# Attention values in split passes over two batches and two heads, with the context sums stored in DRAM between

## The reference

```
q = rmsnorm(layernorm(x) @ Wq); k = rmsnorm(ctx @ Wk); v = ctx @ Wv
attn = softmax(q k^T / sqrt(128)); out = (attn @ v) @ Wo
x = x + out
x = x + ffn(layernorm(x))      # Hadamard rotation, 8-bit activations, ternary weights
```

## Time and profile before

| | us |
|---|---|
| median of 3 runs (1493.36 to 1501.02) | 1493.83 |
| the profiled execution's own time | 1490.84 |
| its span | 1489.1 |
| PE busy in the span | 1419.2 (95%) |
| ACT busy | 986.5 (66%) |
| DVE busy | 940.7 (63%) |
| POOL busy | 521.8 (35%) |

### The profile page before, as it was taken

How to read it: one execution, slowest core, us unless ns; L and a number is a source line. 1 busy time by engine, 2 the same in 40 slices (tenths; PEclk the granted TensorE clock), 3 DMA queues, 4 the chain that set the end, 5 groups by cost and what they waited for, 6 DMA issues and landing times. The chain is left out here.

```text
span 1489.1 us, 30811 instructions
## 1 busy us (share of the span) xinstructions
PE 1419.2 (95%) x9026; PEld 1222.3 (82%) x9026; DVE 940.7 (63%) x2592; ACT 986.5 (66%) x2223; POOL 521.8 (35%) x323
## 2 busy tenths in 40 slices
PE   6999989999999999999999999998699999999996
PEld 6888869999999989899899899997566777677763
DVE  5312046667777777677677777766466777677764
ACT  5556658888888888788788788887434344434442
POOL 0033325422323323332233222235245555455533
PEclk9999989999999999999999999999899999999998
DMA  7767622344434344334333334334611112112100
GB/s 243 215 176 201 192 69 81 102 118 119 113 110 113 112 128 114 102 118 121 118 112 111 109 113 128 102 85 142 216 50 36 42 56 70 42 42 56 49 8 15
DMA packets 160329, 158.26 MB, mean 106 GB/s; under 512 B 83585, under 2 KB 134801, under 8 KB 158417
## 3 DMA queue, kind: packets, MB, share of 16 engines
q1 hardware_dynamic: 153296, 144.40, 34.2%
q10 hardware_dynamic: 6912, 12.59, 2.7%
HBM read 123.44 MB, written 33.14 MB: 105 GB/s over the span
## 5 line engine op out<-in xcount | busy, mean ns | idle before, releaser
L695 POOL TENSOR_TENSOR rk_sp<-ms_sp,neg_half 76x10 f32<-76x10 f32 (+1 forms) x128 | 241.9, 1911 | 605.8 <-DMA ms_sp<-ms 605.8
L848 ACT ACTIVATE k_hi<-psK 128x362 fp32r<-128x362 f32 x256 | 120.5, 471 | 116.6 <-PE psK L729 114.6
L860 ACT ACTIVATE ex<-sc,nb,rq 100x361 f32<-100x361 f32 x256 | 175.6, 686 | 31.7 <-DVE nb L1023 30.3
L729 PE MATMUL psK<-cT_hi,wk_hi 128*128 128x362 f32 x512 | 170.8, 334 | 1.1 <-DVE k_lo L984 1.1
L729 PE MATMUL psK<-cT_hi,wk_lo 128*128 128x362 f32 x512 | 169.0, 330 | 0.0
L729 PE MATMUL psK<-cT_lo,wk_hi 128*128 128x362 f32 x512 | 168.9, 330 | 0.0
L995 DVE TENSOR_TENSOR pT_lo<-psP,pT_hi 121x300 fp32r<-121x300 f32 x256 | 120.4, 470 | 73.8 <-ACT pT_hi L875 69.8
L867 ACT ACTIVATE pr<-ex,ri 100x361 f32<-100x361 f32 x256 | 153.0, 598 | 13.7 <-PE psP L764 13.6
L1016 DVE CUSTOM_DVE_ANT_0 sc<-psS,rk 100x361 f32<-100x361 f32 x256 | 135.5, 529 | 19.4 <-PE psS L753 13.6
L776 PE MATMUL psZ<-pT_hi,cK_hi 120*128 120x400 f32 (+1 forms) x384 | 143.1, 373 | 0.1
L984 DVE TENSOR_TENSOR k_lo<-psK,k_hi 128x362 fp32r<-128x362 f32 x256 | 135.7, 530 | 8.6 <-ACT sq L854 8.6
(11 more groups left out here) (172 smaller groups left out, 3530.9 us busy)
## 6 DMA issues: line engine op xcount, KB each, us to landing
rk<-rk_dram SPq DMA_DIRECT2D x64, 564.1 KB
o_in<-o_dram SPq DMA_DIRECT2D x13, 1024.0 KB, 5.8
q_dram<-q_out SPq DMA_DIRECT2D x64, 200.0 KB, 4.3
q_in<-q_dram SPq DMA_DIRECT2D x64, 200.0 KB, 4.8
o_dram<-o SPq DMA_DIRECT2D x64, 200.0 KB, 5.3
stage<-in_w_ff SPq DMA_DIRECT2D x12, 1024.0 KB, 6.1
w_in<-in_w_ff ACTq DMA_DIRECT2D x48, 256.0 KB, 3.0
cT_in<-in_ctxT SPq DMA_DIRECT2D x16, 361.0 KB, 4.9
```

The costliest lines, as they stand in the source:

```text
L695: nc.gpsimd.tensor_tensor(rk_sp[:, cols], ms_sp[:, cols], neg_half[0:HG * SKR, :].to_broadcast([HG * SKR, n]), op=ALU.pow).then_inc(g_rk, 1)
L729: last = nc.tensor.matmul(psK[h % 2][:, 0:SKP], w[:, c, col:col + D], x[:, slot, c, :], start=(n == 0), stop=(n == 3 * CC - 1))
L848: nc.scalar.activation(k_hi[:, j, h, :], psK[h % 2][:, 0:SKP], ACT.Copy)
L860: nc.scalar.activation(ex[:, h % 2, :], sc[:, h % 2, :], ACT.Exp, bias=nb[:, h % 2:h % 2 + 1], scale=rq[:, j % 2, h:h + 1], accum_out=rs[: ...
```

## The change

The values are computed as three F32R passes, from z and Wv both split. For all units but those of the last two batches (`STORED = 56` units), z no longer goes straight to PE. It is stored to a DRAM tensor `z_dram`, ordered by pair of batches, head, partition and batch. When both batches of a pair are stored, each unit of the next pair (8 units, `PAIR`) loads two heads of both batches (`z_in`, 128 x 800), splits them (`z_hi`, `z_lo`), and one matmul covers 200 columns: one head, two batches. The last 8 units are split and multiplied for one batch and four heads, 100 columns at a time, beside the last 6 stored ones; there the code is written with other places (`late(u)`, from unit 58 on). Wv is loaded and split in two pieces in the first group of `queries`, with the stage buffer that the other weights use. Some memory is shared to make room (`squares_mem`), and `dynamic_dma_scratch_size` is set to 512.

The core of the diff:

```diff
+    z_dram = nc.dram_tensor("z_dram", [B // 2 - 1, H, P, 2, CC * SQ], F32, kind="Internal").ap()
...
-        SPLIT_AT = {0: 1, 2: 2, 4: 3, 8: 4, 10: 5}
+        SPLIT_AT = {0: 1, 2: 2, 4: 3, 8: 4, 10: 5, 12: 6, 14: 7}
...
-                        if h == 9:
-                            sp.dma_start(wv_sb[:], wv.rearrange("(c p) n -> p c n", p=P)).then_inc(d_wv, 16)
+                        if h in (9, 11):
+                            load_piece(6 + h // 2 - 4)
...
-        z = sb("z", [P, CC, UQ])
+        z = sb("z", [P, HG, CC, SQ])
+        z_in = sb("z_in", [P, 2, 2, CC, SQ])
+        z_hi, z_lo = (sb(n, [P, 2, 2, CC, SQ], F32R) for n in ("z_hi", "z_lo"))
...
+        def z_free(eng, w):
+            if isinstance(w, int) and w > STORED:
+                eng.wait_ge(v_zlo, of_unit(w - 1) + 1)
+            elif due(w):
+                eng.wait_ge(d_z, w * 16)
...
+            def store_z(u, pair, k):
+                dst = z_dram[bass.ds(held(sp, pair), 1), k % NG * HG:(k % NG + 1) * HG, :, k // NG, :].rearrange("a h p n -> p (a h) n")
+                done = held(sp, u + 1)
+                sp.wait_ge(a_z, done)
+                sp.wait_ge(v_z, done)
                 apart(sp, sp_passed)
-                sp.dma_start(dst, o[:, j % 2, :].rearrange("p (h q) -> p h q", q=SQ)).then_inc(d_o[j % 2], 16)
...
+            def load_z(u, pair, k):
...
+                stored = held(sp, pair * (PAIR * 16) + (NG + k // 2 + 1) * 16)
+                used = held(sp, of_pair(u - 1) + 1)
+                first = isinstance(u, int) and u == PAIR
+                sp.wait_ge(d_z, stored)
+                apart(sp, sp_passed)
+                if not first:
+                    sp.wait_ge(v_zlo, used)
+                apart(sp, sp_passed)
+                sp.dma_start(z_in[:].rearrange("p h b c q -> p h (b c q)"), src).then_inc(d_zin, 16)
...
+                if real(u - 2, STORED):
+                    store_z(u - 2, pair + (k - 2) // PAIR, (k - 2) % PAIR)
+                if not late(u) and real(u + 2 - PAIR, STORED):
+                    load_z(u + 2, pair + (k + 2) // PAIR - 1, (k + 2) % PAIR)
                 if real(u + 2, UNITS):
                     load_q(u + 2, b + (j + 2) // NG, (j + 2) % NG)
                     spread_rk(u + 2, j % 2)
-                if real(u - 2, UNITS):
-                    store_o(u - 2, b + (j - 2) // NG, (j - 2) % NG)
+                if late(u) and real(u + 2 - PAIR, STORED):
+                    load_z(u + 2, pair + (k + 2) // PAIR - 1, (k + 2) % PAIR)
+                if real(u - PAIR, STORED):
+                    store_pair(u, pair - 1, k)
+                if late(u):
+                    store_unit(u - 2, b + (j - 2) // NG, (j - 2) % NG)
...
+            def values(e, heads, width):
+                pe.wait_ge(v_zlo, e + 1)
+                if due(e):
+                    pe.wait_ge(a_o, e)
...
+                for i, head in enumerate(heads):
+                    first = True
                     for c in range(CC):
-                        last = nc.tensor.matmul(psV[:, h * SQ:(h + 1) * SQ], wv_sb[:, c, col:col + D],
-                                                z[:, c, h * SQ:(h + 1) * SQ], start=(c == 0), stop=(c == CC - 1))
-                    if h == HG - 1:
-                        last.then_inc(p_v, 1)
...
+                        for w, x in ((wv_hi, hi), (wv_hi, lo), (wv_lo, hi)):
+                            last = nc.tensor.matmul(psV[:, i * width:(i + 1) * width], w[:, c, head * D:(head + 1) * D],
+                                                    x[:, i, :, c, :], start=first, stop=(c == CC - 1 and w is wv_lo))
+                            first = False
+                last.then_inc(p_v, 1)
...
+                    if h == 0 and real(u - PAIR, STORED):
+                        values(of_pair(u), (2 * k, 2 * k + 1), 2 * SQ)
+                    if h == 2 and late(u):
+                        values(of_unit(u - 2), range((j - 2) % NG * HG, (j - 2) % NG * HG + HG), SQ)
...
             def copy_z(u):
                 act.wait_ge(p_z, u * CC + 1)
-                if due(u):
-                    act.wait_ge(p_v, u)
-                nc.scalar.activation(z[:, 0, :], psZ[0][:, 0:UQ], ACT.Copy).then_inc(a_z, 1)
+                z_free(act, u)
+                nc.scalar.activation(z[:, :, 0, :], psZ[0][:, 0:UQ].rearrange("p (h q) -> p h q", q=SQ), ACT.Copy).then_inc(a_z, 1)
...
+            def high_z(e, part):
+                if due(e):
+                    act.wait_ge(p_v, e)
+                nc.scalar.activation(z_hi[:].rearrange("p h b c q -> p (h b c q)"), part, ACT.Copy).then_inc(a_zhi, 1)
...
+                    if h == 0 and late(u):
+                        high_unit(u - 2)
+                    if h == (3 if late(u) else 0) and real(u + 1 - PAIR, STORED):
+                        high_pair(u + 1)
...
+                    if h == 1 and late(u):
+                        low_z(of_unit(u - 2), z[:].rearrange("p h c q -> p (h c q)"))
+                    if h == (3 if late(u) else 2) and real(u + 1 - PAIR, STORED):
+                        low_z(of_pair(u + 1), z_in[:].rearrange("p h b c q -> p (h b c q)"))
```

More of the change, by code:

```diff
@@ L171, in queries @@
             pieces.append((wk.rearrange("(c p) n -> p c n", p=P)[:, :, cols], wk_hi[:, :, cols], wk_lo[:, :, cols]))
+        for j in range(2):
+            cols = slice(j * KWD, (j + 1) * KWD)
+            pieces.append((wv.rearrange("(c p) n -> p c n", p=P)[:, :, cols], wv_hi[:, :, cols], wv_lo[:, :, cols]))
         halves = [slice(k * QW // 2, (k + 1) * QW // 2) for k in range(2)]
@@ L294, in squares @@
                     rows = slice(j * QW32, (j + 1) * QW32)
-                    last = nc.tensor.matmul(psS[rows, 0:GT], sel[:, QW32 - 1 - k:2 * QW32 - 1 - k], sq[:, k % 2, j, :],
+                    last = nc.tensor.matmul(psS[rows, 0:GT], sel[:, QW32 - 1 - k:2 * QW32 - 1 - k], sq[k % 2][:, j, :],
                                             start=(k == 0), stop=(k == NG - 1), tile_position=(0, j * QW32))
@@ L517, in attention @@
     CHUNKS = 3 * WC * FF // DIM
+    STORED = UNITS - 2 * NG
+    PAIR = 2 * NG
     with ExitStack() as ctx:
@@ L521, in attention @@
         cT_in, cK_in = weights["cT_in"], weights["cK_in"]
-        cT_hi, cT_lo, ones = (weights[k] for k in ("cT_hi", "cT_lo", "ones"))
+        cT_hi, cT_lo = (weights[k] for k in ("cT_hi", "cT_lo"))
         cK_hi, cK_lo = sb("cK_hi", [P, 2, 3, CD], F32R), sb("cK_lo", [P, 2, 3, CD], F32R)
@@ L573, in pipeline, with batch, late, of_pair @@
         def pipeline(eng, unit):
-            def batch(b, par):
+            def batch(pair, par):
+                b = pair * 2 + par
                 for j in range(NG):
-                    unit(b * NG + j, b, j, par)
+                    unit(b * NG + j, b, j, par, pair)
             for b in range(-1, 4):
-                batch(b, b % 2)
+                batch(b // 2, b % 2)
             with eng.Fori(2, B // 2 - 1) as pair:
[L582 to L585, removed]
+                batch(pair, 0)
+                batch(pair, 1)
+            batch(B // 2 - 1, 0)
+            batch(B // 2 - 1, 1)
             for j in range(2):
-                unit(UNITS + j, B, j, 0)
+                unit(UNITS + j, B, j, 0, B // 2)
+        LAST_ONE = STORED + 2
+        def late(u):
+            return isinstance(u, int) and u >= LAST_ONE
+        def of_pair(u):
+            return u - PAIR if not late(u) else LAST_ONE - PAIR + 2 * (u - LAST_ONE)
+        def of_unit(w):
+            return of_pair(min(w + 2, UNITS - 1)) + 1 + max(w + 3 - UNITS, 0)
+        def z_free(eng, w):
[3 more added lines that the diff above has]
+                eng.wait_ge(d_z, w * 16)
         def first_batch(b):
@@ L644, in unit @@
+            def unit(u, b, j, par, pair):
                 if j == 0 and real(b, B - 1):
@@ L817, in unit @@
                         gather(u - 1, (j - 1) % NG, par if j else 1 - par, h - 2)
-            nc.tensor.matmul(psV[:, 0:3], ones[:], asums[:], start=True, stop=True).then_inc(p_sum, 1)
+            pe.wait_ge(g_ones, 1)
+            nc.tensor.matmul(psV[:, 0:3], o[:, 0, 0:P], asums[:], start=True, stop=True).then_inc(p_sum, 1)
             pipeline(pe, unit)
```

129 lines of the change are left out of this document (78 added, 51 removed).

## The result

The changed kernel takes 1711.82 us (median of 4 runs, 1705.77 to 1714.29) against 1493.93 for the one before on the same chip: 1.144 times the time, 95% interval 1.1417 to 1.1464. Predicted were 1664 us and 1525 to 1730. The profiled execution has a span of 1711.2 us, 222.1 more than before.

A forecast was written before the change was run, and what follows sets the result against it. It took the two-unit ring through z's store to bound the kernel at 16.15 us a unit. 1489.1 + 148 + 13 + 6 + 3 = 1659, plus 1.7 and 3.0, gave 1664 us; range 1525 to 1730.

The forecast's parts named there:

- The value matmul: On PE, 12 records of 200 columns at 0.112 us in a stored unit: 1.34 us instead of 1.79, 0.45 less.
- the line: Record distances on PE at 256 and 512 columns, extended down to 200 columns: 0.094 us a record.
- The rival of slow short passes: One-pass matmuls of 200 columns on PE take some 0.39 us each, giving 1726 us; chance 0.06.
- the ring: Z's copy, split, load, SP chain, store and landing: 32.3 us over two units, 16.15 each, +148 us; chance 0.72.
- The landing of the store: On SP's queue, the 400 KB store of z was taken to need 5.9 us to land.
- PE stays the bound: Z's copy never waits and PE bounds: 1470 us at 0.094 a record, 1493 at 0.112; chances 0.08 and 0.04.
- The turn-taking rival: Stores land in time; alternating ACT and DVE bound units at 13.5 us, 35 more, 1528 us; chance 0.10.
- The last units: Units 58 to 63 pay 2.2 us each on PE, 13; two half-empty units behind them add 6.
- The start: In the first group of queries, two more splits of Wv wait for staged loads: 3 us, bounds 0 and 10.

The follow-up runs named there:

- e2: Changed kernel with only the store of z moved, from behind SP's whole chain to between the issue of ms_sp and the wait for POOL: 1626.8 us.
- e3: Changed kernel with the store of z issued by ACT at head 1 on ACT's own DMA queue: 1638.4 us.
- e4: Changed kernel with z's load behind the rk chain, both splits of z at the end of head 3, and z's store ahead of the POOL wait: 1727.7 us.
- e11: The kernel before the change with 4 of 8 value matmuls left in each unit: 1482.8 us, ratio 0.990–0.993.
- e9: e8 with 4 of the 12 value matmuls left in each two-batch pass: 1596.5 us.
- e8: e5 with load_z moved from behind the rk chain to behind the early store, ahead of SP's wait for POOL: 1586.0 us.
- e10: e8 with load_z put back behind the rk chain for the last eight units alone: 1566.0 us.
- e12: e10 with the stored pairs' high and low splits on POOL at h = 2, in all but the last units: 1536.4 us.
- e7: Changed kernel with 8 of the 24 value matmuls left in each one-batch pass of the last eight units: 1684.8 us.
- e5: e4 with ACT's high split of the stored pair moved to the start of head 3: 1597.1 us.
- e6: e2 with ACT's high split of the stored pair at the start of head 3, for the last eight units only: 1621.9 us.

## Why the prediction was right, and where not

**The value matmul: right.** 0.112 us was taken for 200 columns, against 0.094 by the line; measured 0.111. The same pace at 100 and at 200 columns says what rows of before could not: the moving columns do not set it. What these records have in common is the load of 128 x 128 weights; that this load sets the pace is argued, not shown by itself. The rival of slow short passes (0.39 us) is out. Its sum had a slip that matters: 4.7 - 1.8 is 2.9 us a unit and not 3.2, which makes 1711 us, the measured time. So the time alone could not have told it from the ring; the distances of the records and e2 do. The Trainium skill, TensorE: Matmul & The Clock Gate, section LDWEIGHTS (loading the stationary operand), estimates 107 ns for such a load; the trace agrees at 2.4 GHz with 0.111 us, and not at 1.2 GHz, where the pace is 0.213. Nor does it agree for the transposes `psX`: they load 128 columns too, in 100 rows, and follow one another at 0.086 us (median of 59 distances at a clock of 1.00).

**The ring: right.** 16.15 us a unit forecast, 16.25 measured, +149 us against +148. Its signs came as named: `z` idle with the DMA of `z_dram` as releaser (125 us in 44 times, 2.8 each, where I had 4), SP waiting for `z_lo`, POOL's powers 5.7 us behind the issue of `ms_sp`, PE at 86% (I had near 80%). e2 and e3 cut it and get 85 and 73 us. The landing of the store, 5.9 taken, was 5.6. The estimate of 2.9 us from the Trainium skill, DMA: Bandwidth & Descriptors, section Anatomy of one DMA — SWDGE (gpsimd) path, which is about DMAs that GpSimd issues, is about half of that. But e4's store, with nothing issued shortly ahead of it, meets it:

```profile
z_dram<-z SPq DMA_DIRECT2D x56, 400.0 KB, 2.7
```

So the prediction's reason against the estimate (half the bytes never land under 4.7 us) was a reading of that store's place in the queue, behind the load of `rk`, and not of its bytes. In the changed kernel the store of `z` stands behind that load too, so the 5.9 held. Two small slips of the sum change nothing: the low ends of the ring add up to 29.6 us and not 29.4, the high ones to 35.6 and not 36.

**The premise that PE had room to give: wrong, without a cost to the forecast.** I wrote that fewer microseconds on PE shorten a unit. e11 shows that of such a gain about a fifth comes through (12.6 of 57). Its most frequent unit takes 12.7 us, and the idle time of ACT before `ex` for DVE's `nb` doubles from 13.7 to 27.0 us (300 to 940 us), so the turns of ACT and DVE are what binds there, as far as the waits say. So the rival "PE stays the bound", 1470 us, could hardly have come true even without the ring, and e9 shows no gain from less work on PE in the arrangement of e8. The turn-taking rival had its size right: 13.5 us a unit forecast, 13.70 in e8, 13.76 in e10; e12 shows that the splits on ACT and DVE make up the surplus.

**The last units: the term that was mis-sized.** I put 13 + 6 = 19 us, "36 x 0.112 = 4.03 instead of 1.79"; it is +60, or +57 from the first scores of unit 58. The step that failed is the price at full clock, with nothing else lost. The eight bursts of 24 short passes take 30.3 us from first to last start (2.6 to 4.9 each), where 0.112 gives 20.6: about half of the distances are 0.213 us. That is 10 of the 41 us that were missing. e7 takes 16 of the 24 away in each of the eight and gets 27 us back by the medians, 23 by the profiled ends: under half of the 60. In the late window the clock is 0.82 and PE is busy 81%, so all its other matmuls are slower too, and it stands between them. An estimate from that row: a mean of 0.82 between 0.5 and 1.0 means 52 of the 143.7 us at the lower level, which costs PE at most 26 us, the 10 of the short passes among them. The late split has its part of some 10 us (e5, e6, e10 and e12 against the others). e8 against e10 shows that the place of `load_z` is worth 20 us here by the medians, 13 in the ends. How the 60 divide between clock and waits is open.

**The start: mis-sized too.** 3 us with bounds of 0 and 10; it is +13.1. Of these, 7.9 us stand already at the first copy of `rq` (211.9 instead of 204.0 us), inside the bounds of 0 and 10, and 2.7 came between the copies for units 6 and 7, where by the prediction the ring first closes. Two waits of the first part are longer or new, PE for `xT_lo` 5.3 us (1.8 before) and ACT for the staged Wv 3.0:

```profile
PE psQ L327 <- DVE xT_lo L464: 5.3, 3, 2.9
...
ACT wv_hi L358 <- DMA stage<-in_wv: 3.0, 2, 2.0
```

No run took this part alone, and in the variants with the same start it was +3 to +10, so a part of it varies from one execution to the next. These two errors, 41 and 10, and 1 in the ring are the 52 us between the forecast for the span (170 more) and the 222 measured; of the medians, 1664 and 1712, it is 48, since the profiled execution of before lay 3.0 us under its median and that of the changed kernel 2.5 above.

## What to carry to other kernels

A single buffer that one unit stores and the next overwrites makes the store's place in its queue part of the loop: go round the ring (copy, work up to the split, load, chain, store, landing), divide by the units that it spans, and issue the store where the queue stands idle anyway. An operation split over two engines was best placed at the start of the first engine's turn and at the end of the second's; one line in the wrong place cost 131 us here. A busy share of 99% did not show that the engine's work was worth its length: taking work away, and nothing else, did (12.6 of 57 us).

## What the runs showed of the hardware

- Split passes with 128 x 128 weights follow one another at 0.111 us at 2.4 GHz and 0.213 at 1.2, at 100 and 200 columns alike. So a pass of half the columns saved nothing.
- After stands of PE of some 4 us its clock was at the lower level (4.34 us, then 0.50 in the window). A wait of ACT can so be paid a second time on PE: the loop's clock is 0.93 with the ring, 0.90 with e4's link (330 to 1100 us), and 0.98 in e5, e8 and e12 (330 to 1060 us). In e9 less work for PE went with a lower clock, 0.76 against 0.84, and a longer time; why is open.
- What the store of 400 KB took to land went with what was issued ahead of it on the queue. The median is 5.6 us in the changed kernel, where `rk`, `o` and a weight are issued in the 2.6 us ahead; 4.1 in e2, behind `z_in`, `q_in` and `ms_sp`; and 2.7 in e4, where in the unit looked at nothing was issued in the 9 us ahead.
- POOL's splits in e12 lengthen DVE's subtraction `q_lo`, which has both inputs in SBUF: from 568 to 996 ns in the mean (330 to 1060 us; the rows are e10's and e12's). The 24 of its `q_lo` that meet no work of POOL take 557 to 568 ns, those that meet POOL's splits up to 1704. The copy of `rq`, also in SBUF, took 1.88 us three times instead of 0.16, each time beside POOL's `z_lo`. Subtractions that read PSUM kept theirs beside the same work: `k_lo` 531 and 528, `pT_lo` 466 and 468.

```profile
L1085 DVE TENSOR_TENSOR q_lo<-q_in,q_hi 128x400 fp32r<-128x400 f32 x52 | 29.5, 568 | 0.0
```

```profile
L1102 DVE TENSOR_TENSOR q_lo<-q_in,q_hi 128x400 fp32r<-128x400 f32 x54 | 53.8, 996 | 0.0
```
